# The expert-weight table of the last stage: a masked outer product of exponentials in place of eight one-hot rows

## The reference

```python
queries = (hidden_states @ W_q).reshape(2, n, 64)
routing = jnp.einsum('tnd,tdk->tnk', queries, keys)      # two sides of 64 keys
scores2, idx2 = jax.lax.top_k(routing, 8)
all_scores = (sx[:, :, None] + sy[:, None, :]).reshape(n, 64)
all_idx = (ix[:, :, None] * 64 + iy[:, None, :]).reshape(n, 64)
scores, pk = jax.lax.top_k(all_scores, 8)
indices = jnp.take_along_axis(all_idx, pk, axis=-1)
de, ue = down_embed[indices], up_embed[indices]          # 512 rows each; an index above 511 reads row 511
ew = jax.nn.silu(einsum(x, de)) * jax.nn.softmax(scores, axis=-1)
out = silu(x @ gate_w) * (x @ up_w) @ down_w + einsum(ew, ue)
```

## Time and profile before

| what | value |
|---|---|
| median of three runs | 1088.12 us (1087.78 to 1089.84) |
| the profiled execution: its own time, its span | 1089.05 us, 1087.3 us |
| busy over the span: PE, DVE, ACT, POOL | 988.2, 558.1, 362.9, 265.9 us |
| mean granted TensorE clock | 0.945 of full |
| last stage | from about 949 us; last matmul starts by 1082.82 us, last `add` at 1084.75 us |

### The profile page before, as it was taken

The page is one execution under the profiler, slowest core; times in us unless marked ns, Lnnn a source line. Parts: engine busy times, 40 slices in busy tenths (PEclk is TensorE's granted clock), DMA queues, the critical chain, the costliest instruction groups (busy, mean ns, idle before and its releaser), DMA issues.

```text
span 1087.3 us, 18561 instructions
## 1 busy us (share of the span) xinstructions
PE 988.2 (91%) x7228; PEld 697.2 (64%) x7228; DVE 558.1 (51%) x1277; ACT 362.9 (33%) x687; POOL 265.9 (24%) x337
## 2 busy tenths in 40 slices
PE   5888999989999999968874999999679999998989
PEld 4775699546766667657663999999633343453467
DVE  6786423445435344465376112112177878557792
ACT  4672233232122222214210211111014656645750
POOL 5331442410000000022531222221252444202350
PEclk9896999999999999989985999999968999999999
DMA  9103033211011010045012866567112100020000
GB/s 275 53 2 107 18 99 88 83 54 31 19 36 40 26 40 11 6 141 159 2 53 88 295 206 238 204 239 259 64 52 110 54 2 1 2 78 0 1 11 30
DMA packets 39997, 88.96 MB, mean 82 GB/s; under 512 B 4712, under 2 KB 27592, under 8 KB 36584
## 3 DMA queue, kind: packets, MB, share of 16 engines
q1 hardware_dynamic: 32520, 73.60, 20.1%
q0 software_dynamic: 4080, 11.15, 3.7%
q10 hardware_dynamic: 3312, 3.02, 0.8%
HBM read 76.35 MB, written 11.40 MB: 81 GB/s over the span
## 4 chain that ended last, share of the span: by engine, by line
PE 72%; DVE 16%; DMA 3%; issue 3%; ACT 2%; POOL 2%; SPq 1%; DVEq 0%; ACTq 0%; POOLq 0%
PE bank L358 20%; PE bank L1323 10%; PE bank L1342 7%; PE bank L1667 6%; PE bank L2389 5%; PE bank L2414 3%; PE bank L2435 3%; PE bank L1313 3%; PE bank L2884 2%; PE bank L1678 2%; PE bank L1643 2%; PE bank L2453 1%; DVE big L2671 1%; DVE big L2244 1%; DMA big<-yg,big 1%
## 5 line engine op out<-in xcount | busy, mean ns | idle before, releaser
L358 PE MATMUL bank<-XNT,big 128*128 128x512 f32 x296 | 138.5, 618 | 5.5 <-DVE big L2624 4.0
L1323 PE MATMUL bank<-big 128*128 128x128 f32 x1012 | 118.5, 277 | 0.2 <-DMA big<-m_gu 0.2
L1323 PEld LDWEIGHTS bank<-big 128*128 128x128 f32 x1012 | 116.5, 194 | 0.6 <-issue 0.5
L274 POOL TENSOR_TENSOR rstd<-ve,half 128x1 f32<-128x1 f32 x48 | 27.9, 584 | 302.3 <-DVE ve L268 302.1
L358 PEld LDWEIGHTS bank<-XNT,big 128*128 128x128 f32 x296 | 55.8, 195 | 69.8 <-issue 61.2
L2389 PE MATMUL bank<-big,xs 32*128 32x512 f32 x256 | 88.6, 732 | 12.4 <-DVE xs L285 10.5
L2244 DVE TENSOR_REDUCE big<-bank 128x2 f32<-128x512 f32 x128 | 81.9, 685 | 20.7 <-PE bank L2389 20.2
L1101 DVE TENSOR_TENSOR big<-big,bank 128x640 f32<-128x640 f32 x23 | 18.9, 822 | 136.8 <-ACT big L1211 136.8
L1342 PE MATMUL bank<-big 128*128 (+1 forms) x368 | 87.2, 380 | 1.1 <-DVE big L1108 0.7
L2335 ACT ACTIVATE big<-bank 128x1024 f32<-128x1024 f32 x64 | 64.9, 1024 | 40.0 <-PE bank L2414 39.7
L1342 PEld LDWEIGHTS bank<-big 128*128 128x128 f32 (+1 forms) x368 | 66.3, 190 | 9.0 <-issue 1.9
(11 more groups left out here) (356 smaller groups left out, 1752.5 us busy)
## 6 DMA issues: line engine op xcount, KB each, us to landing
big<-m_gu SPq DMA_DIRECT2D x23, 1408.0 KB, 6.1
big<-m_d SPq DMA_DIRECT2D x8, 768.0 KB
big<-a_qk SPq DMA_DIRECT2D x16, 256.0 KB, 2.9
yg<-big ACTq DMA_DIRECT2D x23, 128.0 KB, 2.1
big<-m_gu SPq DMA_DIRECT2D x8, 352.0 KB
big<-a_o SPq DMA_DIRECT2D x16, 128.0 KB, 2.1
xn<-XNT SPq DMA_DIRECT2D x8, 256.0 KB, 2.1
big<-f_keys SPq DMA_DIRECT2D x1, 2048.0 KB, 10.9
```

What stands on the lines that cost most here:

```text
L274: e.tensor_tensor(k.rstd[at % NT][:, :], k.ve[at % NT][:, :], k.half[:, 0:1], ALU.pow).then_inc(k.ln_rstd, 1)
L358: ins = e.matmul(out, a, b, start=start and n == 0, stop=stop and n == len(pairs) - 1)
L1323: ins = e.matmul(gu[:, n if n <= WHOLE else n + 1], gu_slot[s % SLOTS][:, c:c + P], xgT[s % 2][:, kb, :], start=kb == 0, stop=kb == KB - 1)
```

## The change

An expert number of 64 a + b below 511 has a below 8, so the dense table of unnormalised weights of a tile is the outer product of the exponentials e0 of the first eight keys of side 0 and e1 of all 64 keys of side 1 (8 by 64 = 512). `less` subtracts the side's largest score; one Exp over `powers` (80 numbers for each tile, 640 in all) takes the place of two over 32; `weights` normalises. For each tile `dense_row(u)` marks the chosen places (match_replace puts -1 where a row of 519 numbers equals one of the eight ix), multiplies out the dense table, keeps it under the mark (scalar_tensor_tensor), and copies the weight of expert 511, which is summed by itself since indices above it are cut to it, into the last column. All of it is VectorE's; ScalarE's `hot` and GpSimd's sums are gone. `places` is split in two (`picked` is its second part), `product(4)` stands ahead of `sides(1)`, and weights are made once for both halves.

```diff
-    MINE, SETS = 4, (0, 2, 6)
+    SETS, AWAY = (0, 2, 6), TOP - 1
...
-    away = [W.take(NE) for _ in (0, 1)]
-    iota, eight = W.take(NE), W.take(TOP)
-    m0, m1, m8, ex = [W.take(NT, TOP) for _ in range(4)]
+    iota, eight = W.take(NE + AWAY), W.take(TOP)
+    m0, m1, m8 = [W.take(NT, TOP) for _ in range(3)]
+    powers = W.take(NT, 2 * TOP + K)
+    ex, e0, e1 = powers[:, :, 0:TOP], powers[:, :, TOP:2 * TOP], powers[:, :, 2 * TOP:]
+    marked, dense = W.take(NE + AWAY), W.take(NE)
+    is_last, last = W.take(NT, TOP), W.take(NT)
     i0, i1, pk = [W.take(NT, TOP, dt=U32) for _ in range(3)]
     f0, f1, fk, fa, fb = [W.take(NT, TOP) for _ in range(5)]
-    w8, ix, nix = [W.take(NT, TOP) for _ in range(3)]
+    w8, ix = [W.take(NT, TOP) for _ in range(2)]
     sm, ri = W.take(NT), W.take(NT)
     alls = W.take(UB, TOP, TOP)
     pick = W.take(UB, TOP, TOP)
-    OB = [A2.take(TOP, NE) for _ in (0, 1)]
+    table = [A2.take(NE) for _ in (0, 1)]
...
-    masks0 = k.count_masks(2)
+    masks0 = k.count_masks(3)
...
-        for t in (1,):
-            if t == 1:
-                e.iota(iota, pattern=[[1, NE]], base=0, channel_multiplier=0, allow_small_or_imprecise_dtypes=True)\
-                    .then_inc(k.masks, 1)
-                e.iota(eight, pattern=[[1, TOP]], base=0, channel_multiplier=0, allow_small_or_imprecise_dtypes=True)\
-                    .then_inc(k.masks, 1)
-        for u in range(NT):
-            ob = OB[u % 2]
-            e.wait_ge(S["oh"], MINE * u + 4)
-            e.tensor_tensor(ob[:, 0:2], ob[:, 0:2], ob[:, 2:4], ALU.add).then_inc(S["sum"], 1)
-            e.wait_ge(S["sum"], 2 * u + 1)
-            e.tensor_tensor(ob[:, 0], ob[:, 0], ob[:, 1], ALU.add).then_inc(S["sum"], 1)
+        e.iota(eight, pattern=[[1, TOP]], base=0, channel_multiplier=0, allow_small_or_imprecise_dtypes=True)\
+            .then_inc(k.masks, 1)
+        e.iota(iota[:, 0:NE], pattern=[[1, NE]], base=0, channel_multiplier=0, allow_small_or_imprecise_dtypes=True)\
+            .then_inc(k.masks, 1)
+        e.memset(iota[:, NE:], NE - 1.0).then_inc(k.masks, 1)
...
-            e.tensor_tensor(ex[:, r], m8[:, r], bc(m8[:, r, 0], 2, TOP), ALU.subtract).then_inc(S["top"], 1)
+            ins = e.tensor_tensor(ex[:, r], m8[:, r], bc(m8[:, r, 0], 2, TOP), ALU.subtract)
+            if b == 0:
+                ch.mark(ins)
+            else:
+                ins.then_inc(S["top"], 1)
...
+        def less(first, m, side):
+
+            for h in (0, 1):
+                ch.mark(e.tensor_tensor(first[:, h::2], rs[:, h, :, side:side + first.shape[2]],
+                                        bc(m[:, h::2, 0], 2, first.shape[2]), ALU.subtract))
...
+        def picked(b):
+            r = slice(UB * b, UB * b + UB)
             for at, f in ((fa, f0), (fb, f1)):
                 ch.step(e.tensor_tensor(pick, bc(at[:, r], 3, TOP), bc(bc(eight, 1, TOP), 1, UB), ALU.is_equal))
                 ch.step(e.tensor_tensor(pick, pick, bc(f[:, r], 2, TOP), ALU.mult))
                 ch.step(e.tensor_reduce(at[:, r], pick, AX.X, ALU.add))
             ch.step(e.scalar_tensor_tensor(ix[:, r], fa[:, r], float(K), fb[:, r], ALU.mult, ALU.add))
             ch.step(e.tensor_scalar(ix[:, r], ix[:, r], NE - 1.0, None, ALU.min))
-            e.wait_ge(S["exp"], b + 1)
-            ch.mark(e.tensor_scalar(nix[:, r], ix[:, r], -1.0, None, ALU.mult))
-            ch.step(e.tensor_reduce(sm[:, r], ex[:, r], AX.X, ALU.add))
-            ch.step(e.reciprocal(ri[:, r], sm[:, r]))
-            e.tensor_tensor(w8[:, r], ex[:, r], bc(ri[:, r], 2, TOP), ALU.mult).then_inc(S["ix"], 1)
-
-        def hot(u):
-            e.wait_ge(S["ix"], u // UB + 1)
+
+        def weights():
+            e.wait_ge(S["exp"], 1)
+            ch.mark(e.tensor_scalar(is_last, ix, NE - 1.0, None, ALU.is_ge))
+            ch.step(e.tensor_reduce(sm, ex, AX.X, ALU.add))
+            ch.step(e.reciprocal(ri, sm))
+            ch.mark(e.tensor_tensor(e0, e0, bc(ri, 2, TOP), ALU.mult))
+            ch.step(e.tensor_tensor(w8, ex, bc(ri, 2, TOP), ALU.mult))
+            ch.step(e.tensor_tensor(is_last, is_last, w8, ALU.mult))
+            ch.step(e.tensor_reduce(last, is_last, AX.X, ALU.add))
+
+        def dense_row(u):
+
+            ch.mark(e.match_replace(out=marked, in_to_replace=ix[:, u], in_values=iota, imm_value=-1.0))
+            ch.step(e.tensor_tensor(dense.rearrange("p (i j) -> p i j", j=K), bc(e0[:, u], 2, K), bc(e1[:, u], 1, TOP), ALU.mult))
             if u >= 2:
                 e.wait_ge(S["wt_ps"], u - 1)
-            for c in range(MINE, TOP):
-                ch.mark(e.tensor_scalar(OB[u % 2][:, c], iota, ix[:, u, c:c + 1], w8[:, u, c:c + 1], ALU.is_equal, ALU.mult))
-
-        def hot_sum(u):
-            ob = OB[u % 2]
-            ch.wait()
-            ch.step(e.tensor_tensor(ob[:, 4:6], ob[:, 4:6], ob[:, 6:8], ALU.add))
-            ch.step(e.tensor_tensor(ob[:, 4], ob[:, 4], ob[:, 5], ALU.add))
-            e.wait_ge(S["sum"], 2 * u + 2)
-            e.tensor_tensor(ob[:, 4], ob[:, 4], ob[:, 0], ALU.add).then_inc(S["w"], 1)
+            ch.step(e.scalar_tensor_tensor(table[u % 2], marked[:, 0:NE], 0.0, dense, ALU.is_lt, ALU.mult))
+            e.tensor_copy(table[u % 2][:, NE - 1:NE], last[:, u:u + 1]).then_inc(S["w"], 1)
...
-        for b in (0, 1):
-            sides(b)
-            product(3 * b + 1)
-            both(b)
-            product(3 * b + 2)
-            places(b)
-            product(3 * b + 3)
-        hot(0)
+        e.wait_ge(k.masks, masks0 + 3)
+        sides(0)
+        product(1)
+        both(0)
+        product(2)
+        places(0)
+        product(3)
+        picked(0)
+        product(4)
+        sides(1)
+        less(e0, m0, 0)
+        less(e1, m1, K)
+        product(5)
+        both(1)
+        product(6)
+        places(1)
+        picked(1)
         product(7)
-        hot_sum(0)
+        weights()
+        dense_row(0)
         product(IB)
-        hot(1)
+        dense_row(1)
         product(IB + 1)
         weighted(0)
-        hot_sum(1)
+        dense_row(2)
...
-        def exp(b):
-            r = slice(UB * b, UB * b + UB)
-            e.wait_ge(S["top"], b + 1)
-            e.activation(ex[:, r], ex[:, r], ACT.Exp).then_inc(S["exp"], 1)
-
-        def hot(n, pair):
-
-            for m in range(n, n + pair):
-                u, c = m // MINE, m % MINE
-                if c == 0:
-                    e.wait_ge(S["ix"], u // UB + 1)
-                    if u >= 2:
-                        e.wait_ge(S["wt_ps"], u - 1)
-                if m >= 2:
-                    e.wait_ge(S["oh"], m - 1)
-                e.activation(away[m % 2], iota, ACT.Abs, bias=nix[:, u, c:c + 1]).then_inc(S["near"], 1)
-            for m in range(n, n + pair):
-                u, c = m // MINE, m % MINE
-                e.wait_ge(S["near"], m + 1)
-                e.activation(OB[u % 2][:, c], away[m % 2], ACT.Relu, bias=w8[:, u, c:c + 1], scale=-2.0)\
-                    .then_inc(S["oh"], 1)
+        def exp():
+            e.wait_ge(S["top"], 1)
+            e.activation(powers, powers, ACT.Exp).then_inc(S["exp"], 1)
...
-        silu(1)
-        silu(2)
-        exp(0)
-        silu(3)
-        silu(4)
-        hot(0, 2)
-        silu(5)
-        exp(1)
-        silu(6)
-        hot(2, 2)
+        for n in range(1, 7):
+            silu(n)
+        exp()
         silu(7)
-        hot(4, 2)
-        silu_e(0)
-        silu_e(1)
-        hot(6, 2)
-        silu_e(2)
-        silu_e(3)
-        silu(IB)
-        silu(IB + 1)
-        for n in range(2, IB):
+        for n in range(EB):
+            silu_e(n)
+        for n in range(IB):
             silu(IB + n)
-            hot(2 * n + 4, 2)
         for n in range(EB):
             silu_e(EB + n)
...
-                ins = e.transpose(bank[:, WT + u % 2, b * P:(b + 1) * P], OB[u % 2][:, 4, b * P:(b + 1) * P], k.ident[:, :])
+                ins = e.transpose(bank[:, WT + u % 2, b * P:(b + 1) * P], table[u % 2][:, b * P:(b + 1) * P], k.ident[:, :])
```

More of the change, by code:

```diff
@@ L2529, in peer_mlp @@
     pick = W.take(UB, TOP, TOP)
-    OB = [A2.take(TOP, NE) for _ in (0, 1)]
+    table = [A2.take(NE) for _ in (0, 1)]
     names = ("ld", "xd", "xp", "q_ps", "q_sb", "k_ps", "r_sb", "g_ps", "silu", "h", "e_ps", "e_sb", "top", "exp",
-             "ix", "near", "oh", "sum", "w", "wt_ps", "he", "o_ps", "st")
+             "w", "wt_ps", "he", "o_ps", "st")
     S = {n: k.sem("p7_" + n) for n in names}
     g = k.dram
-    masks0 = k.count_masks(2)
+    masks0 = k.count_masks(3)
     TURN, QB, WT, OUT = 4, 6, 4, 6
@@ L2695, in dve @@
         e.wait_ge(S["r_sb"], 2)
-        e.wait_ge(k.masks, masks0 + 2)
-        for b in (0, 1):
-            sides(b)
-            product(3 * b + 1)
-            both(b)
-            product(3 * b + 2)
-            places(b)
-            product(3 * b + 3)
-        hot(0)
+        e.wait_ge(k.masks, masks0 + 3)
[15 more added lines that the diff above has]
+        picked(1)
```

(56 more changed lines are left out.)

## The result

The changed kernel took 1075.22 us (median of four, 1073.97 to 1077.14), the kernel before beside it 1087.95 (1087.04 to 1089.84): ratio 0.9871, 95% interval 0.9849 to 0.9892. The direction and the mechanism were forecast; the size was not. The forecast gain was 10.9 us with 8.1 to 12.9 as its range. The ratio says 14.0, above the range (its interval, 11.8 to 16.4 us, reaches into it but not down to 10.9), and the two medians are 12.7 apart, just inside it. Over all executions timed in this study the medians are 1075.8 (14 of the changed kernel, 1072.9 to 1078.6) and 1088.5 (84 of the kernel before, 1084.6 to 1094.4), 12.7 us apart.

A forecast was written before the change was run, and what follows sets the result against it. TensorE's work plus its holes was taken to bound the last stage: 4.03 (first hole) + 1.95 (clock) + 4.96 (tables) = 10.9 us, so 1088.12 - 10.9 = 1077.2 us (chance 0.78), range 1075.2 to 1080.0.

The forecast's parts named there:

- The signs: Last stage: two TensorE holes of about 0.7 us left, `gate_up(8)` near 993, `down(0)` near 1030.4, granted clock 1.00 from 972.
- The chain to `product(7)`: VectorE's first-half steps: `product(7)` starts near 987.9, ends at 988.62, 0.30 us before `embed(2)` needs it.
- the 1078.4 us: Time if the skill's drain of about 1380 ns joins the table switch: `product(7)` 1.2 us too late for `embed(2)`.
- Tables lead by over 7 us: Second half: every table ready over 7 us before its turn, so holes of 0.92, 0.61 and 2.64 us go.
- C: Rival: first hole stays because `embed(1)` or `(2)` waits several us; only the tables' holes go, 1083.2 us; chance 0.03.
- D: Rival: MATCH_REPLACE8 costs by match value, not column; slower, 1100 us at 1 us for each value; chance 0.02.
- E: Rival: no change, the holes only move; chance 0.02.
- B: Rival: `product(7)` late for `embed(2)`, price 0.2 to 1.5 us, 1077.4 to 1078.7 us; chance 0.15.
- the tables' part: Gain from `turn_w(2)` to `down(0)`, from the table holes that go: 4.96 us.
- the first half's: `gate_up(8)` starts 5.98 us earlier: the 4.03 us hole ahead of `embed(1)` plus 1.95 us behind it.
- 1.95 us come back: Without the 4.03 us hole, the twelve instructions behind it keep 2.4 GHz: 5.16 us instead of 7.11.
- 1.00 (2.4 GHz) across the hole of 2.64: Granted clock read as undiminished across the 2.64 us hole ahead of `turn_w(4)`.

The follow-up runs named there:

- `late_seven`: Changed kernel with weights(), seven short steps, ahead of product(7) instead of behind it: 1078.51 us, stage 127.3.
- `replace_x4`: Changed kernel with each row's match_replace done four times, 2.1 us more of VectorE for each tile: 1075.44 us, stage 124.5.
- `late_table`: Changed kernel with table 4 made behind product(15) and seven useless passes of 128x512 ahead of it: 1080.57 us, stage 129.1.
- `before_again`: Kernel before, unchanged, timed against itself: 1089.49 to 1087.87 us, ratio 1.0018, stage 136.3.
- `before_third`: Kernel before, unchanged, profiled a third time: 1089.99 us, ratio to itself 1.0016, stage 138.25.
- `hole_back`: Changed kernel with product(6) put behind picked(1) and four useless passes of 128x512, so that embed(1) waits for it: 1081.61 us, stage 131.0.
- `old_order`: Changed kernel with the first half of the stage in the order of the kernel before: 1079.81 us, stage 127.3.

## Why the prediction was right or wrong

- **Bound, order, chain: right.** TensorE's stream plus its holes was the end, before and after. The signs came: two holes of 0.69 us, `gate_up(8)` 44.4 us behind the start of the stage for 44.3, `down(0)` 81.9 for 81.6. The chain to `product(7)` was 39.25 us for 39.17; its lead was thin as said, and `late_seven` and `replace_x4` show what stands behind it.
- **New operations: right.** Replace 0.70 forecast, 0.684 measured; Exp 0.75 and 0.74; a masked product 0.69; `weights` 1.5 and 1.5. A table switch is the load alone.
- The drain that the Trainium skill adds to a switch (ScalarE: Activation LUTs, What ACT_TABLE_LOAD costs) is in no profile of the last stage here (in the profile after `silu(6)` ends 0.02 us ahead of the load, and the Exp starts 0.01 us behind its end); the 1078.4 us worked out from it did not come.
- **Tables lead by over 7 us: right**, 7.0 at the least; `replace_x4` shows that 2.1 us of it can be spent for each tile. Rivals C, D and E did not come. B's late `product(7)` is there in two profiles (1.48 us in `replace_x4` and in the profile of `late_table`), both times in place of the 1.8 us of slow clock that TensorE did not have, so that it costs the stage nothing.
- **The sum in the stage of the profile shown: right**, 10.9 against 11.1, though the tables' part was 4.8 and not 4.96, the first half's 5.9 and not 5.98, and the 0.3 us behind `down(0)` were missing.
- **The term that failed is the clock**, "1.95 us come back", together with "1.00 (2.4 GHz) across the hole of 2.64" in the earlier trace rows. Both were read from one execution and taken for a property of the kernel, the second also in rival B ("a hole of up to 2.64 left the clock at 1.00"). Of the 1.95, 1.7 are the clock and the rest refill. In three profiles of the kernel before the stage took 135.6, 136.3 and 138.3 us, mean 136.7; the changed kernel took 124.5 in all three. So what the change removes in the stage is 11.1, 11.8 or 13.8 us, mean 12.2, for the 10.9 of the sum. The difference between the three is slow clock: 0.75 us more behind the first hole in `before_again`, 3.0 behind the hole of 2.64 in `before_third`. What a hole cost in these profiles is itself and its refill plus 0 to 3 us of slow clock, and the execution shown was on the cheap side, though its total time (1089.05) lay above the median.
- **All executions say the same.** Each has a span and a mean granted clock; span times one less that clock is an estimate of the time that the slow clock took. Its mean is 57.4 us for the kernel before (80 executions of the runs above) and 52.6 for the changed kernel (14): 4.7 us less, with a standard error of 1.1, where the sum has 1.7. What is left of the spans differs by 8.3 us (standard error 0.7), where the sum has 9.2, holes and refill. So the holes were sized about rightly, and the clock's term was too small. The estimate covers the whole kernel: how much of the 4.7 lies ahead of the stage it can't say.
- **The median of 12.7** is then within 0.5 us of the mean of the stages. Three profiles are few for that mean, and one of them (1092.66 us in all) is among the slower executions. The 14.0 of the first ratio is more than any stage gain seen; the later batches gave 12.7 and 12.4, and no profile shows the part above 13.8. The starts of the stage in the three profiles of each kernel, 948.4 and 946.8 on average, differ by 1.6 us in the same direction; over all fourteen profiles it is 948.1 for the four built on the kernel before and 946.3 for the ten built on the changed one, while one kernel's starts lie up to 3.5 us apart. Whether a part of it is real was not settled.
- **The range** allowed for more cost than the sum and for hardly more gain. The bound below should have come from pricing each hole with the clock lost behind it, as the 4.03 us hole had been: with 2 to 3 us for the second half, down to 1074.
- **What I undervalued** is the GpSimd. I had its overlap in the chain as one row; leaving out its additions alone gives 7.5 of the 11.1 us. The changed kernel has 3.6 more, from a new way of making the table, a free ScalarE and a new order together; and it still makes the whole table, which the run without the additions does not.

## What to carry to other kernels

Price a hole of TensorE as its length plus the slow clock that can follow it, and take the second from several executions: a hole of 2 to 3 us showed it in one profile and not in another. When a GpSimd operation and VectorE share a stage, time the kernel with the GpSimd operation left out: its additions here held VectorE up for nearly as long as VectorE would have needed for them (whether moving them to VectorE would have paid was not run). And when a single profile agrees with a sum to 0.2 us while the medians differ by 2, look first at the term that varies from one execution to the next.

## What the hardware showed that I had not expected

- The clock behind 32 small matmuls (64x64) fell in some executions (0.57 from 960 to 964 us in the profile after) and in others not (1.00 in `hole_back`, `late_seven`, `replace_x4`, `old_order`, `late_table` and `before_again`, six of fourteen profiles). For the kernel before, unchanged, it fell in two of three.
- Holes of 2.15 us (`old_order`) and 2.64 us (`before_third`) were followed by a clock of 0.57; one of 2.64 in the first profile of the kernel before, one of 2.66 in `before_again` and one of 1.48 in `replace_x4` were not.
- MATCH_REPLACE8 took 0.684 us for 519 columns against eight values, as long as a plain two-input pass over 512.
